# Golden weights in four pieces, constants moved, expert rows added by the gathers

## The chip, the cores and the metric

One Trainium2 chip, one of its cores. The metric is device microseconds of one launch; the kernel before takes 431.03 us as the median of three runs (430.78 to 431.78). Times in the text are microseconds from the start of the profiled span unless they say otherwise.

## The reference, cut to what matters

A decoder of two layers over 4 x 256 tokens of width 256. Each layer has an attention, a cross step and a feed-forward step, and after each of them x = layernorm(x + step(x)). Four things matter here.

In the first layer the cross step is a choice of one of four experts by the token's id; only the second half of the tokens (1024 in all, in two halves of 512) is routed through blocks of rows in the kernel:

```
for e in range(E):
    g = silu(einsum('bsd,fd->bsf', hidden_states, Wg[e]))
    u = einsum('bsd,fd->bsf', hidden_states, Wu[e])
    y = einsum('bsf,df->bsd', g * u, Wd[e])
    out = where((expert_ids == e)[..., None], y, out)
```

The feed-forward step of the first layer has eight experts (256 wide), all of them computed for all tokens, and summed by the Golden weights, eight small numbers for each token:

```
inh = sigmoid(x @ Wr / temperature)
in_zone = (inh >= GOLDEN_LOWER) & (inh <= GOLDEN_UPPER)
distance = abs(inh - GOLDEN_CENTER)
weights = exp(-distance / 0.1) * in_zone
no_expert = sum(weights) < 1e-08
fb = exp(-distance / 0.3)
fb_w = fb * (mask of fb's two largest);  fb_w = fb_w / max(sum(fb_w), 1e-08)
weights = where(no_expert, fb_w, weights)
weights = weights / max(sum(weights), 1e-08)
out = einsum('bte,betd->btd', weights, e_out)
```

The second layer's attention works in groups of 32 tokens, its cross step is a masked attention over ctx (the mask is one of the constants below), and its feed-forward step has eight routed experts of 176 and a shared one.

## The kernel before, in words

**Tiles.** Tokens lie in eight tiles of 128 (x_tok, 128 partitions x 256 each), four tiles to a half (HT = 4). Every matmul operand is kept as two float32r parts, high and low, and a product is three matmuls: high x high, high x low, low x high. So each weight pack (pk_raw, loaded by SyncE) is rounded by ScalarE into pk_hi and the rest is taken by GpSimd into pk_lo; each hidden block (hraw) goes the same way into h_hi and h_lo.

**Units and slots.** A unit is one expert for one half of the tokens: units 0 to 3 are the four experts of the first layer's cross step (first half of the tokens), 4 to 11 the Golden experts for the first half, 12 to 19 those for the second half. Each unit has two slots of 128 hidden rows; slot 8 is the first of unit 4. For a slot TensorE makes the gate product (step g, 6 matmuls of 128x512) and the up product (step u, also 6); ScalarE takes the Silu (s, L1233); VectorE multiplies (m, L1888); ScalarE rounds (h, L1247); GpSimd subtracts (l, L1489). After two slots TensorE makes the down product (d, 24 matmuls of 128x256, L877 to L879) into banks 4 and 5, and VectorE adds it to x_tok with the unit's weights (a, four instructions, L1902). ScalarE and GpSimd convert a unit's gate and up weights in step G (L1265, L1495) and its down weights in step D (L1276, L1500).

**The waits around it.** u of a slot waits for m of two slots earlier, since it writes the bank that this m reads. g waits for the Silu of two slots earlier. d waits for the low halves of both of its slots and, bank by bank, for the two adds of the unit before it that read this bank. A pack's high half waits until TensorE has used the buffer it goes to.

**Orders.** Each engine runs a list written out by hand (PE_ORDER, ACT_ORDER, POOL_ORDER, DVE_ORDER, SP_ORDER): a name of a step and its number, in program order. There is no other scheduling; an engine that waits holds all that is behind it. r0.i and r1.i are the steps of the Golden routing for the first and second half: 0 the layernorm's statistics, 2 the transposes' low parts, 3 the logits, 4 the distance (VectorE) and the two exps (ScalarE), 5 the whole of the Golden weights (VectorE, gold_weights). gold_weights is a chain of small instructions (128x32 or 128x4), each linked to the one before by a semaphore: zone, near weights, the two largest with their masks (top2), the fallback, the sum of both. Its result gold is read by the adds a4 and later (first half), a12 and later (second half). Its neighbours in DVE_ORDER are m9 and m10 in the first half and m24 and m25 in the second.

**The cross step's blocks.** The second half's tokens are sorted by expert into seven blocks of 128 rows in DRAM (xs_dram) by indirect DMAs (steps P), go through the experts block by block (steps x1.0j to x1.4j, x1.4j being the statistics of the first half's tiles), and lie in ys_dram. Four indirect DMAs, issued by GpSimd (steps Q, x0_fetch), gather each token's row into o_tok; VectorE adds a tile of them to x_tok and takes the layernorm's statistics (x1.50 to x1.53). k1 to k4 are the small VectorE steps that compute the slots; k4 makes the list of the blocks' experts, which TensorE reads ahead of x1.10.

**Constants.** Step c (later_constants, L1766 to L1770) casts the pad mask to float (128x1024), takes its maximum, scales it, and makes bk_four; the first reader is the second layer's attention.

Of the kernel before, what the change touches and what calls it, by code (L numbers as in the profile page):

```python
# [183 lines left out]
e0.10 e1.10 m24 r1.5 m25 e0.12 e1.12 m26 c a0.3 a12 a0.4 m27 a0.5 a0.6 m28 a0.7 m29 a0.8 a13 m30 a0.9 a0.10 a14 m31
a0.25 m32 m33 a0.11 e0.0 a15 a0.26 e1.0 m34 a16 e0.2 e1.2 m35 e0.3 e1.3 m36 e0.4 e1.4 m37 e0.5 e1.5 m38 a17 m39 e0.7
e1.7 a18 a0.22 a19 e2.10 e3.10 a0.23 m40 e2.12 e3.12 a1.3 a1.4 m41 m42 a1.5 a1.6 a1.7 a1.8 o43 m43 a1.9 o44 m44 a1.10
a1.25 o45 m45 o46 m46 a1.11 o47 m47 a1.26 e2.0 e3.0 o48 m48 e2.2 e3.2 e2.3 e3.3 o49 m49 o50 m50 e2.4 e3.4 e2.5 e3.5
o51 m51 o52 m52 e2.7 e3.7 o53 m53 a1.22 a1.23 m54 x0 m55 m56 o57 m57 o58 y0 m58 o59 m59 o60 m60 o61 m61 o62 m62 o63
m63 o64 m64 o65 m65 o66 m66 o67 m67 w0 w1 z1
""".split()  # L190


def decoder_program(nc, x_rows, x_cols, ids, pad_mask, w_attn0, w_attn1, bias_cols, bias_rows, bias_v1, bias_o,
                    w_route, temperature, consts, pk_x0, pk_f0, pk_x1, pk_f1, cw_dram, xs_dram, ys_dram, out):
    with ExitStack() as ctx:
# [3 lines left out]
        def sem(name):  # L199
# [1206 lines left out]
        def _(pool):  # L1406
# [189 lines left out]
        def _(dve):  # L1596
# [75 lines left out]
            def per_token(v):  # L1672
                return v.unsqueeze(2).to_broadcast([P, HT, E0])
# [64 lines left out]
            def x0_expert(stage, j):  # L1738
# [12 lines left out]
                elif stage == 2:  # L1751
                    dve.wait_ge(sems["x0_hh"], j + 1)
                    TT(h0_cols(h_lo, j), x0_bank(2, j).rearrange("p (c t) -> p c t", c=KC),
                       h0_cols(h_hi, j).bitcast(F32), ALU.subtract).then_inc(sems["x0_hl"], 1)
                elif stage == 4:
                    dve.wait_ge(sems["acc_done"], 4 * (EX - 1) + j + 1)
                    link(dve.bn_stats(stats[:, j, :], x_tok[:, j, :]))
                else:
                    T = HT + j
                    dve.wait_ge(sems[f"x0_got{j // 2}"], 32)  # L1760
                    TT(x_tok[:, T, :], x_tok[:, T, :], o_tok[:, j, :], ALU.add).then_inc(sems["x0_added"], 1)
                    dve.wait_ge(sems["x0_added"], j + 1)
                    link(dve.bn_stats(stats[:, j, :], x_tok[:, T, :]))
# [178 lines left out]
            def golden(i, h):  # L1942
# [7 lines left out]
                elif i == 4:  # L1950
# [296 lines left out]
```

## Time and profile before

| | |
|---|---|
| median of three runs | 431.03 us |
| the profiled execution | 432.45 us |
| its span | 430.4 us |
| mean granted clock of TensorE | 0.992 |
| busy: PE / PEld / DVE / ACT / POOL | 95% / 82% / 60% / 56% / 63% of the span |
| chain that ended last | PE 71%, DVE 14%, ACT 5%, issue 4%, POOL 2%, DMA 2% |

PE is TensorE (PEld its weight loads), DVE VectorE, ACT ScalarE, POOL GpSimd; L12 is line 12 of the kernel. A timeline row gives start, duration and, in brackets, how long the engine had been idle and what released it. An instruction that stands in its engine waiting for a resource, and not for a semaphore, shows this as a longer duration. A matmul's end is modelled: the row of a product that follows on can begin a little before the one ahead has ended. The granted clock is the share of the 2.4 GHz level that TensorE was given. The profile comes from one execution, so a sum made in it is made against 432.45 us.

### The profile page before, as it was taken

Reading aid. Unit: us, or ns where it says so; the run is one execution under the profiler, and the core shown is the slowest. Engines: PE = TensorE matmul, PEld = TensorE weight load, DVE = VectorE, ACT = ScalarE, POOL = GpSimd, SP = SyncE. Lnnn points to the kernel's source line nnn. Section 1 sums busy time; section 2 is a strip of 40 time slices with the busy share of each in tenths; the row PEclk is TensorE's granted clock in tenths of the full one; section 3 lists DMA queues with packets and bytes.
Section 4 is the critical chain, followed back from the end, with each engine's and each line's share of the span. In section 5 each row is a group of like instructions: output and inputs, shape, how many; then the busy total and the mean of one; then the engine's idle time right before and its main releaser. Section 6 shows DMA issues by size and latency. Waiting matters only on the chain.

```text
span 430.4 us, 9389 instructions
## 1 busy us (share of the span) xinstructions
PE 409.0 (95%) x3615; PEld 354.7 (82%) x3615; DVE 257.2 (60%) x652; ACT 239.6 (56%) x429; POOL 271.3 (63%) x251
## 2 busy tenths in 40 slices
PE   8999999995999999899989999999989999999994
PEld 6888979884889888788878899798768989888983
DVE  5868757529836348966644587656445676363243
ACT  4846664673384775352733757672635757544543
POOL 2744484374598577575867548457757386877763
PEclk9999999999999999999999999999999999999998
DMA  7843022413023313042232102222532332554412
GB/s 248 288 143 116 36 68 80 148 51 122 0 79 124 105 61 124 24 126 96 76 89 76 38 0 84 68 98 62 145 116 75 115 104 79 155 161 151 140 31 99
DMA packets 22855, 43.09 MB, mean 100 GB/s; under 512 B 3051, under 2 KB 10347, under 8 KB 22812
## 3 DMA queue, kind: packets, MB, share of 16 engines
q1 hardware_dynamic: 21708, 40.92, 30.2%
q0 software_dynamic: 384, 1.05, 0.7%
q8 instruction: 29, 0.48, 0.5%
q10 hardware_dynamic: 720, 0.53, 0.4%
q14 instruction: 14, 0.11, 0.1%
HBM read 38.52 MB, written 3.44 MB: 97 GB/s over the span
## 4 chain that ended last, share of the span: by engine, by line
PE 71%; DVE 14%; ACT 5%; issue 4%; POOL 2%; DMA 2%; SPq 0%; DVEq 0%; POOLq 0%; ACTq 0%
PE bank L548 12%; PE bank L549 11%; PE bank L551 11%; PE bank L877 6%; PE bank L879 6%; PE bank L878 6%; PE bank L957 3%; DVE hraw L1888 2%; PE bank L896 2%; PE bank L945 1%; DMA q_buf<-x_cols_dram 1%; DVE x_tok L1902 1%; POOL rstd L1419 1%; PE bank L571 1%; PE bank L927 1%
## 5 line engine op out<-in xcount | busy, mean ns | idle before, releaser
L1489 POOL TENSOR_TENSOR h_lo<-hraw,h_hi 128x512 fp32r<-128x512 f32 x68 | 87.7, 1293 | 65.7 <-ACT h_hi L1247 65.5
L548 PE MATMUL bank<-xT_hi,pk_hi 128*128 128x512 f32 x240 | 97.8, 408 | 6.3 <-DVE hraw L1888 6.3
L549 PE MATMUL bank<-xT_hi,pk_lo 128*128 128x512 f32 x240 | 95.2, 397 | 0.6 <-issue 0.6
L1247 ACT ACTIVATE h_hi<-hraw 128x512 fp32r<-128x512 f32 x68 | 42.8, 629 | 75.3 <-DVE hraw L1888 75.2
L551 PE MATMUL bank<-xT_lo,pk_hi 128*128 128x512 f32 x240 | 76.0, 398 | 0.0
L1495 POOL TENSOR_TENSOR pk_lo<-pk_raw,pk_hi 128x512 fp32r<-128x512 f32 (+1 forms) x44 | 74.6, 1695 | 1.5 <-ACT pk_hi L1265 1.3
L1888 DVE TENSOR_TENSOR hraw<-bank,sil 128x512 f32<-128x512 f32 x68 | 46.9, 689 | 47.1 <-ACT sil L1233 22.6
L877 PE MATMUL bank<-pk_hi,h_hi 128*128 128x256 f32 x240 | 68.9, 287 | 0.2
L879 PE MATMUL bank<-pk_hi,h_lo 128*128 128x256 f32 x240 | 67.8, 283 | 0.0
L878 PE MATMUL bank<-pk_lo,h_hi 128*128 128x256 f32 x240 | 67.8, 282 | 0.0
L548 PEld LDWEIGHTS bank<-xT_hi,pk_hi 128*128 128x128 f32 x240 | 45.6, 190 | 17.2 <-DVE hraw L1888 7.2
L1500 POOL TENSOR_TENSOR pk_lo<-pk_raw,pk_hi 128x256 fp32r<-128x256 f32 (+1 forms) x44 | 41.9, 952 | 20.5 <-ACT pk_hi L1276 20.5
L551 PEld LDWEIGHTS bank<-xT_lo,pk_hi 128*128 128x128 f32 x240 | 45.4, 189 | 11.1 <-DVE xT_lo L1650 0.3
L549 PEld LDWEIGHTS bank<-xT_hi,pk_lo 128*128 128x128 f32 x240 | 45.7, 190 | 9.6 <-issue 0.9
L877 PEld LDWEIGHTS bank<-pk_hi,h_hi 128*128 128x128 f32 x240 | 45.8, 191 | 1.8 <-issue 0.9
L878 PEld LDWEIGHTS bank<-pk_lo,h_hi 128*128 128x128 f32 x240 | 45.8, 191 | 0.8
L879 PEld LDWEIGHTS bank<-pk_hi,h_lo 128*128 128x128 f32 x240 | 45.8, 191 | 0.0
L1276 ACT ACTIVATE pk_hi<-pk_raw 128x256 fp32r<-128x256 f32 (+1 forms) x44 | 21.5, 489 | 32.4 <-PE bank L879 32.3
L1265 ACT ACTIVATE pk_hi<-pk_raw 128x512 fp32r<-128x512 f32 (+1 forms) x44 | 34.2, 777 | 8.5 <-DMA pk_raw<-pk_f_dram 4.8
L1419 POOL TENSOR_TENSOR rstd<-var_e,mhalf 128x2 f32<-128x2 f32 (+1 forms) x19 | 15.3, 806 | 30.9 <-DVE var_e L1619 22.1
L1902 DVE SCALAR_TENSOR_TENSOR x_tok<-bank,gold,x_tok 128x256 f32<-128x256 f32 x64 | 27.2, 476 | 10.3 <-PE bank L879 10.2
L1233 ACT ACTIVATE sil<-bank 128x512 f32<-128x512 f32 x46 | 27.0, 587 | 6.1 <-PE bank L551 6.0
(306 smaller groups left out, 808.6 us busy)
## 6 DMA issues: line engine op xcount, KB each, us to landing
pk_raw<-pk_f_dram SPq DMA_DIRECT2D x28, 384.0 KB, 3.1
pk_raw<-pk_f_dram SPq DMA_DIRECT2D x16, 512.0 KB, 3.6
pk_raw<-pk_f_dram SPq DMA_DIRECT2D x16, 256.0 KB, 3.3
kv_buf<-pk_x_dram SPq DMA_DIRECT2D x4, 512.0 KB, 3.6
x_tok<-x_rows_dram SPq DMA_DIRECT2D x1, 1024.0 KB, 9.4
pk_raw<-pk_x_dram SPq DMA_DIRECT2D x4, 256.0 KB, 5.8
brow<-cw_dram SPq DMA_DIRECT2D x4, 256.0 KB, 3.2
cw_late<-cw_dram SPq DMA_DIRECT2D x4, 256.0 KB, 3.4
```

Source lines behind the costliest of these rows:

```text
L548: pe.matmul(o, w(kc)[0], x(kc)[0], start=kc == 0, stop=False)
L549: pe.matmul(o, w(kc)[1], x(kc)[0], start=False, stop=False)
L551: m = pe.matmul(o, w(kc)[0], x(kc)[1], start=False, stop=kc == KC - 1)
L877: pe.matmul(o, hh, vh, start=first, stop=False, skip_group_check=True)
L878: pe.matmul(o, hh, vl, start=False, stop=False, skip_group_check=True)
L879: m_ = pe.matmul(o, hl, vh, start=False, stop=closed and t % 2 == 1 and kc == chunks - 1, skip_group_check=True)
L1247: A(h_hi[:, row, at * 512:(at + 1) * 512], hraw[:, s % 2, :], ACT.Copy).then_inc(sems["hid_hi"], 1)
L1265: A(g_part(kind, i, pk_hi), raw, ACT.Copy).then_inc(sems["g_hi"], 1)
L1489: pool.tensor_tensor(h_lo[:, row, q], hraw[:, s % 2, :], h_hi[:, row, q].bitcast(F32), ALU.subtract).then_inc(sems["hid_lo"], 1)
L1495: pool.tensor_tensor(g_part(kind, i, pk_lo)[:, 0:w], raw_g(kind, i)[0][:, 0:w], g_part(kind, i, pk_hi)[:, 0:w].bitcast(F32), ALU.subtract) ...
L1500: pool.tensor_tensor(d_part(kind, i, pk_lo), raw_d(kind, i)[0], d_part(kind, i, pk_hi).bitcast(F32), ALU.subtract).then_inc(sems["d_lo"], 1)
L1888: TT(hraw[:, r, :], other[:, :], sil[:, r, :], ALU.mult).then_inc(sems["hid_mul"], 1)
```

## The change

The Golden weights are cut into four pieces on VectorE: zone goes to the end of step 4, near (with top2) is step 5, fallback step 6 and total step 7. In the first half near stays between m9 and m10, fallback and total go behind x1.50 and x1.51, and a4 goes from behind x1.50 to behind m13. In the second half the three pieces go from between m24 and m25 to behind m21, m22 and m23, ahead of a10. The constants (c) go from behind m26 to behind m18, k4 from ahead of a0 to behind m5. On ScalarE the first half's two exps (r0.4) go from behind G2 to ahead of h8. The four gathers add each token's row to x_tok in the DMA (compute_op add), so o_tok, the four VectorE adds and their semaphore fall away; the statistics now wait for the gather alone. The orders of TensorE, GpSimd and SyncE are the same.

```diff
 ACT_ORDER
-... r0.2 x1.36 s8 r0.3 h8 s9 h9 G2 r0.4 s10
+... r0.2 x1.36 s8 r0.3 r0.4 h8 s9 h9 G2 s10
...
 DVE_ORDER
-k3 m1 n1.0 m2 m3 k4 a0 m4 m5 m6 a1 ...
+k3 m1 n1.0 m2 m3 a0 m4 m5 k4 m6 a1 ...
...
-... r0.2 r0.3 m8 r0.4 m9 r0.5 m10 x1.50
-a4 m11 x1.51 m12 x1.52 x1.53 r1.0 m13 m14 a5 a6 m15 m16 m17 r1.2 a7 r1.3 a8 m18 r1.4 m19 m20 a9 m21 m22 m23 a10 a11
-e0.10 e1.10 m24 r1.5 m25 e0.12 e1.12 m26 c a0.3 ...
+... r0.2 r0.3 m8 r0.4 m9 r0.5 m10 x1.50
+r0.6 m11 x1.51 r0.7 m12 x1.52 x1.53 r1.0 m13 a4 m14 a5 a6 m15 m16 m17 r1.2 a7 r1.3 a8 m18 c r1.4 m19 m20 a9 m21 r1.5
+m22 r1.6 m23 r1.7 a10 a11 e0.10 e1.10 m24 m25 e0.12 e1.12 m26 a0.3 ...
...
             def x0_fetch(t):
 
                 pool.wait_ge(sems["x0_ys"], 16 * NB)
-                pool.indirect_dma_start(o_tok[:, t, :], None, ys_dram,
-                                        bass.IndirectOffsetOnAxis(ap=slot_i[:, t:t + 1], axis=0)
-                                        ).then_inc(sems[f"x0_got{t // 2}"], 16)
+                pool.indirect_dma_start(x_tok[:, HT + t, :], None, ys_dram,
+                                        bass.IndirectOffsetOnAxis(ap=slot_i[:, t:t + 1], axis=0),
+                                        compute_op=ALU.add).then_inc(sems[f"x0_got{t // 2}"], 16)
...
                     T = HT + j
                     dve.wait_ge(sems[f"x0_got{j // 2}"], 32)
-                    TT(x_tok[:, T, :], x_tok[:, T, :], o_tok[:, j, :], ALU.add).then_inc(sems["x0_added"], 1)
-                    dve.wait_ge(sems["x0_added"], j + 1)
                     link(dve.bn_stats(stats[:, j, :], x_tok[:, T, :]))
...
-            def gold_weights(h):
+            def gold_zone(h):
 
                 q = slice(HT * h, HT * (h + 1))
                 dve.wait_ge(sems["rt_dist"], h + 1)
                 link(TS(zone[:, q, :], inh[:, q, :], float(GOLD_LO), None, ALU.is_ge))
                 link(STT(pick[:, q, :], inh[:, q, :], float(GOLD_HI), zone[:, q, :], ALU.is_le, ALU.mult))
+
+            def gold_near(h):
+
+                q = slice(HT * h, HT * (h + 1))
                 dve.wait_ge(sems["rt_exp"], h + 1)
                 link(TT(wz[:, q, :], wz[:, q, :], pick[:, q, :], ALU.mult))
                 total(s1[:, q], wz[:, q, :])
                 link(TS(none_in[:, q], s1[:, q], 1e-8, None, ALU.is_lt))
                 top2(fb, h)
+
+            def gold_fallback(h):
+
+                q = slice(HT * h, HT * (h + 1))
                 link(TT(fb[:, q, :], fb[:, q, :], pick[:, q, :], ALU.mult))
                 total(s2[:, q], fb[:, q, :])
                 link(TS(s2[:, q], s2[:, q], 1e-8, None, ALU.max))
                 link(dve.reciprocal(s1[:, q], s2[:, q]))
                 link(TT(fb[:, q, :], fb[:, q, :], per_token(s1[:, q]), ALU.mult))
                 link(TT(fb[:, q, :], fb[:, q, :], per_token(none_in[:, q]), ALU.mult))
+
+            def gold_total(h):
+
+                q = slice(HT * h, HT * (h + 1))
                 link(TS(s2[:, q], none_in[:, q], -1.0, 1.0, ALU.mult, ALU.add))
                 link(TT(wz[:, q, :], wz[:, q, :], per_token(s2[:, q]), ALU.mult))
                 link(TT(wz[:, q, :], wz[:, q, :], fb[:, q, :], ALU.add))
...
                     STT(dist[:, q, :], inh[:, q, :], float(GOLD_C), zone[:, q, :], ALU.subtract, ALU.max
                         ).then_inc(sems["rt_dist"], 1)
+                    gold_zone(h)
                 elif i == 5:
-                    gold_weights(h)
+                    gold_near(h)
+                elif i == 6:
+                    gold_fallback(h)
+                elif i == 7:
+                    gold_total(h)
```

## Rows read from the trace of the kernel before

**Rows 1.** TensorE's timeline (start us, duration us, engine, line, operation, [idle before it and releaser]).

```profile
95.25 0.36 PE L877 MATMUL bank<-pk_hi,h_hi 128*128 128x256 f32 x1
...
106.33 0.80 PE L548 MATMUL bank<-xT_hi,pk_hi 128*128 128x512 f32 x1 [5.17 <-DVE hraw L1888]
...
114.86 0.28 PE L877 MATMUL bank<-pk_hi,h_hi 128*128 128x256 f32 x1
```

**Rows 2.** Busy time by window: start:end, length, PE, PEld, DVE, ACT, POOL, granted clock, DMA.

```profile
106.30:109.30 3.00, 2.97 (x7) 2.42 (x8) 2.93 (x8) 1.12 (x2) 1.28 (x1) 0.50 0.01 3
```

**Rows 3.** VectorE's timeline around the Golden weights of the first half.

```profile
89.36 0.19 DVE L1954 SCALAR_TENSOR_TENSOR dist<-inh,zone 128x32 f32<-128x32 f32 x1
...
92.27 0.69 DVE L1888 TENSOR_TENSOR hraw<-bank,sil 128x512 f32<-128x512 f32 x1 [2.71 <-ACT sil L1233]
...
96.34 1.07 DVE L1924 TENSOR_TENSOR wz<-wz,pick 128x32 f32<-128x32 f32 x1 [3.07 <-ACT fb L1303]
...
99.28 1.29 DVE L1666 TENSOR_TENSOR pick<-con,top_f 128x32 f32<-128x32 f32 x1
...
101.27 2.10 DVE L1930 TENSOR_SCALAR s<-s 128x4 f32<-128x4 f32 x1
...
105.58 0.69 DVE L1888 TENSOR_TENSOR hraw<-bank,sil 128x512 f32<-128x512 f32 x1
```

**Rows 4.** GpSimd's timeline in the same stretch.

```profile
94.95 2.40 POOL L1495 TENSOR_TENSOR pk_lo<-pk_raw,pk_hi 128x1024 fp32r<-128x1024 f32 x1
...
99.17 1.35 POOL L1500 TENSOR_TENSOR pk_lo<-pk_raw,pk_hi 128x512 fp32r<-128x512 f32 x1 [1.82 <-ACT pk_hi L1276]
...
101.00 2.34 POOL L1495 TENSOR_TENSOR pk_lo<-pk_raw,pk_hi 128x1024 fp32r<-128x1024 f32 x1 [0.48 <-ACT pk_hi L1265]
```

**Rows 5.** Tile o_tok: count, ns min/median/max, first and last start us.

```profile
L1446 POOL DMA_INDIRECT o_tok<-ys_dram,slot_i x4: 947/950/1082, 86.1 to 90.0; - x4
...
L1761 DVE TENSOR_TENSOR x_tok<-x_tok,o_tok x4: 414/415/1491, 106.2 to 112.2; 128x256 f32<-128x256 f32 x4
...
DMA to landing us min/median/max: 1.7/1.9/2.7
```

**Rows 6.** VectorE's timeline, 141 to 159.

```profile
141.16 0.25 DVE L1953 TENSOR_SCALAR zone<-inh 128x32 f32<-128x32 f32 x1
...
153.47 0.69 DVE L1888 TENSOR_TENSOR hraw<-bank,sil 128x512 f32<-128x512 f32 x1 [2.33 <-ACT sil L1233]
...
155.40 0.69 DVE L1888 TENSOR_TENSOR hraw<-bank,sil 128x512 f32<-128x512 f32 x1 [1.24 <-ACT sil L1233]
...
158.77 0.88 DVE L1902 SCALAR_TENSOR_TENSOR x_tok<-bank,gold,x_tok 128x256 f32<-128x256 f32 x2 [0.72 <-PE bank L879]
```

**Rows 7.** GpSimd's timeline, 145 to 157.

```profile
145.27 1.29 POOL L1489 TENSOR_TENSOR h_lo<-hraw,h_hi 128x512 fp32r<-128x512 f32 x1 [2.06 <-ACT h_hi L1247]
...
156.85 1.29 POOL L1489 TENSOR_TENSOR h_lo<-hraw,h_hi 128x512 fp32r<-128x512 f32 x1 [0.65 <-ACT h_hi L1247]
```

**Rows 8.** ScalarE's timeline, the high half of weight pack 3.

```profile
99.86 1.06 ACT L1265 ACTIVATE pk_hi<-pk_raw 128x1024 fp32r<-128x1024 f32 x1 [0.77 <-PE bank L551]
```

**Rows 9.** VectorE's timeline, the constants (first and last of four).

```profile
177.37 0.69 DVE L1766 CAST cap<-mask_w 128x1024 f32<-128x1024 uint8 x1
...
180.07 2.24 DVE L1770 TENSOR_SCALAR bk_four<-con,bcol 128x4 f32<-128x4 f32 x1
```

**Rows 10.** TensorE's timeline, 147 to 176.

```profile
147.19 0.28 PE L877 MATMUL bank<-pk_hi,h_hi 128*128 128x256 f32 x1
...
160.18 0.36 PE L877 MATMUL bank<-pk_hi,h_hi 128*128 128x256 f32 x1
...
175.51 0.50 PE L548 MATMUL bank<-xT_hi,pk_hi 128*128 128x512 f32 x1 [1.15 <-DVE hraw L1888]
```

**Rows 11.** VectorE's timeline, the multiply m4.

```profile
55.54 0.69 DVE L1888 TENSOR_TENSOR hraw<-bank,sil 128x512 f32<-128x512 f32 x1
```

**Rows 12.** ScalarE's timeline, the Silu s4.

```profile
54.86 0.58 ACT L1233 ACTIVATE sil<-bank 128x512 f32<-128x512 f32 x1
```

More of the change, by code:

```diff
@@ L158 @@
 s4 h4 s5 h5 G1 s6 h6 D1 s7 h7 x1.00 x1.01 x1.10 x1.02 x1.11 x1.20 x1.03 x1.12 x1.21 x1.04 x1.30 x1.13 x1.22 x1.05
-x1.31 x1.14 x1.23 x1.06 x1.32 x1.15 x1.24 x1.33 x1.16 x1.25 x1.34 x1.26 x1.35 r0.2 x1.36 s8 r0.3 h8 s9 h9 G2 r0.4 s10
+x1.31 x1.14 x1.23 x1.06 x1.32 x1.15 x1.24 x1.33 x1.16 x1.25 x1.34 x1.26 x1.35 r0.2 x1.36 s8 r0.3 r0.4 h8 s9 h9 G2 s10
 D2 G3 h10 s11 h11 s12 h12 s13 h13 s14 D3 G4 r1.1 h14 s15 S0 D4 G5 h15 s16 h16 s17 r1.2 h17 D5 G6 D6 s18 r1.3 h18 s19
@@ L180 @@
 k0 p2 b0.0 b0.1 b0.2 b0.3 b0.4 b0.5 k1 b1.0 b0.6 b0.7 b1.1 b0.8 p5 b1.2 n0.0 b1.3 b1.4 b1.5 b1.6 b1.7 n0.2 b1.8 k2 m0
-k3 m1 n1.0 m2 m3 k4 a0 m4 m5 m6 a1 m7 a2 x1.00 x1.01 a3 x1.10 x1.02 x1.11 x1.20 x1.03 x1.40 x1.12 x1.21 x1.04 x1.41
+k3 m1 n1.0 m2 m3 a0 m4 m5 k4 m6 a1 m7 a2 x1.00 x1.01 a3 x1.10 x1.02 x1.11 x1.20 x1.03 x1.40 x1.12 x1.21 x1.04 x1.41
 x1.13 x1.22 x1.05 x1.42 x1.14 x1.23 x1.06 x1.43 r0.0 x1.15 x1.24 x1.16 x1.25 x1.26 r0.2 r0.3 m8 r0.4 m9 r0.5 m10 x1.50
-a4 m11 x1.51 m12 x1.52 x1.53 r1.0 m13 m14 a5 a6 m15 m16 m17 r1.2 a7 r1.3 a8 m18 r1.4 m19 m20 a9 m21 m22 m23 a10 a11
[L184 to L189, printed above, removed]
+r0.6 m11 x1.51 r0.7 m12 x1.52 x1.53 r1.0 m13 a4 m14 a5 a6 m15 m16 m17 r1.2 a7 r1.3 a8 m18 c r1.4 m19 m20 a9 m21 r1.5
+m22 r1.6 m23 r1.7 a10 a11 e0.10 e1.10 m24 m25 e0.12 e1.12 m26 a0.3 a12 a0.4 m27 a0.5 a0.6 m28 a0.7 m29 a0.8 a13 m30
+a0.9 a0.10 a14 m31 a0.25 m32 m33 a0.11 e0.0 a15 a0.26 e1.0 m34 a16 e0.2 e1.2 m35 e0.3 e1.3 m36 e0.4 e1.4 m37 e0.5 e1.5
+m38 a17 m39 e0.7 e1.7 a18 a0.22 a19 e2.10 e3.10 a0.23 m40 e2.12 e3.12 a1.3 a1.4 m41 m42 a1.5 a1.6 a1.7 a1.8 o43 m43
+a1.9 o44 m44 a1.10 a1.25 o45 m45 o46 m46 a1.11 o47 m47 a1.26 e2.0 e3.0 o48 m48 e2.2 e3.2 e2.3 e3.3 o49 m49 o50 m50
+e2.4 e3.4 e2.5 e3.5 o51 m51 o52 m52 e2.7 e3.7 o53 m53 a1.22 a1.23 m54 x0 m55 m56 o57 m57 o58 y0 m58 o59 m59 o60 m60
+o61 m61 o62 m62 o63 m63 o64 m64 o65 m65 o66 m66 o67 m67 w0 w1 z1
 """.split()
@@ L312, in decoder_program @@
             x0_t_ps x0_xh x0_xl x0_g_ps x0_silu x0_mul x0_v_ps x0_hh x0_hl x0_d_ps x0_y x0_ys
-            x0_got0 x0_got1 x0_added""".split()
+            x0_got0 x0_got1""".split()
         for n in names:
```

## The prediction

> **How the profile is read.** Steps are named as in the order lists: g and u are a slot's gate and up products on TensorE, d a unit's down product, s the Silu and h the high half on ScalarE, m the multiply and a the adds of a unit on VectorE, l the low half on GpSimd, G and D a weight pack's two conversions (ScalarE, then GpSimd). All moments are those of the trace before.
>
> **What bounds the kernel now.** TensorE is busy 95% of the span, so only its holes can be won. Its timeline has one large hole: u12 begins at 106.33, 5.17 us after g12 ended, and the releaser is the VectorE multiply m10 [rows 1]. The window behind it shows the granted clock at 0.50 for 3.0 us, the 1.2 GHz level [rows 2]; against the 2.4 GHz level that is another 1.5 us. So the hole costs up to 6.7 us in all. From u12 to d5 five products take 8.53 us [rows 1], 7.03 at full clock, 1.41 each.
>
> The hole is the Golden weights of the first half, one piece on VectorE between m9 and m10: from 96.34 to 105.58 [rows 3]. These are 128x32 instructions of 0.19 us, but three of them last 1.07, 1.29 and 2.10 us. Put beside GpSimd's timeline the reason shows: each ends 0.03 to 0.06 us after a GpSimd subtraction ends (97.35, 100.52, 103.34) [rows 4]. An instruction of VectorE that works from SBUF to SBUF waits for the GpSimd instruction that is running; what reads PSUM, and the reductions and searches, did not wait in this trace. I call it a lock. Behind the third stall ten instructions take 2.21 us, so 0.22 each. That prices the new pieces: fallback (6 instructions) 1.3 us, total (7) 1.5, near what is left, 9.24 less the stalls 3.9 less 2.8, so 2.5.
>
> **The change part by part.**
>
> *The adding gathers.* Four VectorE adds go: 0.41 us each, the longest 1.49 because of a lock [rows 5]. That is 2.7 us of VectorE time between 106 and 114. The gathers are issued on GpSimd at 86.1 to 90.0, 0.95 us each, and landed 1.7 to 2.7 us after issue [rows 5]. VectorE asks for them at x1.50, at 99 at the earliest, so their landing may grow by 5 us unseen. What an adding gather costs GpSimd to issue no row shows. The nearest row is the plain one, so 0.95, taken as unchanged; the upper bound is twice that, since it has two operands per row; below nothing there is no reason to go. The queue behind them is l8, l9 and pack 2. The Trainium skill, "Collectives: The Full Stack", section "The bandwidth ceiling: the fold count and why AG ≠ RS ≠ AR", says that the add inside a DMA is free but that it reads two sources and so needs twice the read descriptors. By that page the issue could reach the upper bound, and the time would be that of the rival on the gathers below; no row here shows it.
>
> *The exps ahead of h8 on ScalarE.* They wait for dist, which ends at 89.55 [rows 3], and take two times 0.2 (estimate, the size of that row); h8 could start at about 89.3. So h8, s9 and m9 come 0.65 us later: m9 at 92.9 instead of 92.27. A low half starts 1.45 us after its multiply starts (155.40 to 156.85) [rows 6, 7] and lasts 1.3, so l9 ends at 95.65, and d4, at 95.25 before [rows 1], starts 0.4 later. The fewer table switches are off the path.
>
> *Near, fallback, total of the first half.* Near runs from 93.5. Its first instructions and the searches last to 95.3, the copy waits for l9 (95.65), the next instruction for pack 2's subtraction right behind it (2.40 us [rows 4]), so to 98.05, and near ends at 98.5. m10 takes 98.5 to 99.2; u12 wants it at 101.55. So the hole of 5.17 us and the slow clock go: five products on, d5 could start at 108.6 instead of 114.86, a gain of 6.3.
>
> What is late next? d5 needs half of a4, since a4 frees its bank, and a4 now stands behind fallback, total and m13. The statistics of x1.50 (0.4, like the add of that size) bring VectorE to 99.6. Then GpSimd runs D2 (99.55 to 100.9), pack 3 (101.4 to 103.75, because its ScalarE half starts at 99.86 [rows 8] plus 0.4) and l10 (to 105.0). If fallback meets all three, it ends at 105.05 and m11 with it, 0.7 us too late even for its own start; u13 stands 1.4 us. Total meets l11 (1.45 us behind m11) and ends at 108.75; u14 stands 0.9. Behind m12 come two statistics, the aggregation, l12's lock, m13 at 111.7 and half of a4 (0.88): d5 at 113.25, gain 1.6. If fallback slips ahead of D2 and pack 3, and here 0.05 us decide it, then m11 comes by 103.8, m12 at 107.5, d5 at 112.0, gain 2.9. Between them I take 2.3. VectorE and u14 absorb the 0.4 of d4 in either case.
>
> *Constants moved (c).* Before they ran from 177.37, three instructions in 2.70 us, the fourth then locked to 2.24 [rows 9]; what they cost there was hidden behind d12, so I win nothing. In the new place they stand between m18 and r1.4, which began at 141.16 [rows 6]: 2.7 + 0.2, a short lock of 0.2, then r1.4 0.4 and zone 0.4 put m19 at 145.1. Before, l19 at 145.27 [rows 7] puts m19 at 143.8. l19 now ends at 147.85, and d9, which reads it, began at 147.19 [rows 10]: 0.7 us lost (between 0 and 1.2).
>
> *Near, fallback, total of the second half.* Before they stood behind m24 and cost one wait of 1.15 us before u27 [rows 10]; this goes. Now they stand between m21, m22, m23 and a10. m21 starts at 153.47 [rows 6], near at 154.1; its copy waits for l21 (to 156.2), m22 at 156.8 instead of 155.40. Fallback from 157.4; its last instruction can't pass l22 (158.25 to 159.55), m23 at 159.8. Total from 160.4 meets l23 (161.25 to 162.55) and ends at about 163.1. Only then comes a10, which before began at 158.77 and whose first half takes 0.88 [rows 6]: 164.0. d11 waits for just this half (it began at 160.18 [rows 10]); queued behind d11 on TensorE is everything. Loss 3.7 us; without any lock a10's half is done at 161.5, loss 1.3.
>
> *k4 behind m5.* Its 0.8 us leave the place ahead of m4. But m4 began at 55.54 [rows 11] and its Silu ended at 55.44 [rows 12]: at most 0.1 us, taken as nothing. Behind m5 its cover is the wait for the next Silu; TensorE reads the block list some 10 us later.
>
> **Sum.** -2.3 + 0.7 + 3.7 - 1.15 = +0.95 us. The profiled execution took 432.45, its span 430.4, 2.05 around it; it lies 1.42 above the median. 432.45 + 0.95 = 433.4 there, 432.0 for the median.
>
> **The rivals.** About 0.2%, 0.86 us, is what a measurement can tell from no change.
> - *The pieces meet no locks.* Then near ends at 96.0, m11 hangs only on pack 3, h10 and s11 on ScalarE (102.6), m12 comes at 105.15, half of a4 at 108.7 and d5 at once: -6.1. Second half: +0.5 + 1.3 - 1.15. Together -5.45: 425.6. For it: every lock is a meeting of two timelines that both shift. Against it: GpSimd stands in subtractions for most of 94 to 106, and l follows each m by 1.45 us wherever the pieces lie.
> - *Only the second half is free of locks* (decided by whether l21 to l23 fall on searches and reductions): -2.3 + 0.65 = -1.65: 429.4. Against it: fallback's last instruction starts 1.7 us behind its multiply, inside l22.
> - *The clock falls in d11's wait.* TensorE would stand 3.7 us, and the granted clock fell here after 5.17 us of standing and not after 1.15. If it falls as before, 1.5 us more: 433.5.
> - *The adding gathers hold GpSimd.* From an issue time of 1.4 us up (four times 0.45 is l9's room) they decide: at 1.9 each, l9 ends at 97.4, d4 starts 2.1 us late, of which the later waits give back some 0.6: 433.5.
> - *m10 stays late* and the hole stays, with nothing moved: 431.0.
>
> **How the numbers follow.** Forecast 0.44, of it 0.20 within 0.2% and 0.24 slower, since 0.95 lies just beyond the 0.86; no locks 0.12; second half free 0.17; clock 0.13; gathers 0.12; m10 late 0.02. Faster: 0.12 + 0.17 = 0.29. Within: 0.20 + 0.02 = 0.22. Slower: 0.24 + 0.13 + 0.12 = 0.49. Leaving out the rival without locks (0.12) and some 0.08 at the top, where two of the slower ones meet, the range is 427.8 to 434.4. The forecast alone, by its bounds (first half -2.9 to -1.6, c 0 to 1.2, d11 3.4 to 4.0, less 1.15), spans 430.4 to 433.5.
>
> **What would show it.** Right: no wait before u12 and no window at 0.50 there; waits before u13, u14 and d5 that sum to some 4 us, released by m11, m12 and x_tok adds; a new wait of 3 to 4 us before d11, released by x_tok; none of 1.15 before u27; the longest small VectorE instructions still end with GpSimd subtractions. Wrong: the gathers at over 1.4 us on GpSimd, a d11 that starts behind d10, or a wait for the gathers' landing at x1.50.

## The result, and the profile after

| | before | after |
|---|---|---|
| median | 430.9 us (4 runs, 430.7 to 431.8) | 437.06 us (4 runs, 436.39 to 438.85) |
| ratio, 95% interval | | 1.0145 (1.0111 to 1.018) |
| profiled execution, its span | 432.45, 430.4 | 436.39, 434.4 |
| mean granted clock | 0.992 | 0.990 |

The change costs 6.2 us; 1 us was forecast and the range ended at 434.4. Of all the executions one, the profiled one of experiment 6, ran at a mean granted clock of 0.845 and took 452.36 us; it is left out.

First the two traces must be laid on each other. I call the changed kernel after. In its trace everything on TensorE runs 1.08 us earlier from the first product that waits for loaded weights on; nothing of the change lies ahead of it, and the other kernels below spread over the same range (8.86 to 10.07). The row of before, then that of after (start, duration):

```profile
10.07 0.47 PE L628 MATMUL bank<-wa_hi,xT_hi 128*128 128x512 f32 x1
```

```profile
8.99 0.47 PE L628 MATMUL bank<-wa_hi,xT_hi 128*128 128x512 f32 x1
```

So every moment of after is compared with that of before plus 1.08, and I call the difference the lag. By the spans the change costs 4.0 + 1.08 = 5.1 us in these two executions; before's profiled execution lies 1.5 above its median, and its start, the latest of all, may be the larger part of that.

TensorE's timeline of after, its waits of 0.4 us and more between 90 and 200 us (in brackets how long it was idle, and the releaser):

```profile
95.13 0.35 PE L877 MATMUL bank<-pk_hi,h_hi 128*128 128x256 f32 x1 [0.77 <-POOL h_lo L1489]
...
101.45 0.50 PE L548 MATMUL bank<-xT_hi,pk_hi 128*128 128x512 f32 x1 [0.41 <-DVE hraw L1886]
...
105.98 0.50 PE L548 MATMUL bank<-xT_hi,pk_hi 128*128 128x512 f32 x1 [1.47 <-DVE hraw L1886]
...
109.65 0.50 PE L548 MATMUL bank<-xT_hi,pk_hi 128*128 128x512 f32 x1 [0.61 <-DVE hraw L1886]
...
113.25 0.36 PE L877 MATMUL bank<-pk_hi,h_hi 128*128 128x256 f32 x1 [1.93 <-DVE x_tok L1900]
...
146.26 0.36 PE L877 MATMUL bank<-pk_hi,h_hi 128*128 128x256 f32 x1 [0.44 <-issue]
...
165.11 0.55 PE L877 MATMUL bank<-pk_hi,h_hi 128*128 128x256 f32 x1 [5.87 <-DVE x_tok L1900]
```

In order these are d4, u12, u13, u14, d5, d9 and d11. The hole of 5.17 us before u12 [rows 1] is gone, and a hole of 5.87 us stands before d11. The granted clock around both places (start:end, length, busy time of PE, PEld, DVE, ACT, POOL, clock, DMA):

```profile
110.00:113.40 3.40, 1.47 (x7) 0.93 (x6) 3.33 (x11) 1.80 (x4) 2.81 (x4) 1.00 0.00 0
113.40:116.50 3.10, 3.10 (x26) 3.06 (x27) 2.06 (x6) 0.11 (x2) 0.97 (x1) 1.00 0.00 0
164.75:168.00 3.25, 2.89 (x13) 2.92 (x14) 1.00 (x3) 0.00 (x0) 2.83 (x2) 0.50 0.76 246
168.00:171.00 3.00, 3.00 (x17) 2.86 (x16) 1.41 (x4) 0.47 (x1) 0.00 (x0) 0.65 0.48 175
```

The clock stays up at d5 and falls to the 1.2 GHz level behind d11's wait: d11 lasts 5.3 us instead of 3.1.

The lag along the span: +0.96 at d4; -0.53 at d5, where -2.3 was forecast; +0.15 at d9; and behind d11 (+5.9 for its wait, +2.2 for the clock) +8.2 at g24. Then it shrinks: 0.4 at the transposes ahead of u26, 1.4 at u27, where before waited 1.15 us [rows 10], 0.5 up to g28, and 0.8 over the last 250 us, where the traces differ in short waits, most of them marked issue. That leaves 5.1.

The gathers of after, by their line (count, ns min/median/max, first and last start), beside [rows 5]:

```profile
L1446 POOL DMA_INDIRECT x_tok<-ys_dram,slot_i x4: 1546/1556/1674, 85.1 to 90.8; - x4
...
DMA to landing us min/median/max: 3.7/3.8/3.9
```

An adding gather holds GpSimd for 1.55 us where a plain one took 0.95. DMA packets between 84 and 100 us, before and then after (packets, MB, share):

```profile
q0 software_dynamic: 192, 0.52, 10.5%
```

```profile
q0 software_dynamic: 576, 0.52, 22.6%
```

The same bytes go in three times the packets. In before they are 128 packets of 4 KB and 64 small ones, in after 512 of 1 KB, each a token's row by itself, and the same 64.

Behind the last one, GpSimd's and then VectorE's timeline:

```profile
90.77 1.55 POOL L1446 DMA_INDIRECT x_tok<-ys_dram,slot_i  x1 [0.30 <-issue]
91.76 3.12 POOL L1489 TENSOR_TENSOR h_lo<-hraw,h_hi 128x512 fp32r<-128x512 f32 x2
94.27 2.95 POOL L1495 TENSOR_TENSOR pk_lo<-pk_raw,pk_hi 128x1024 fp32r<-128x1024 f32 x1
```

```profile
92.13 5.16 DVE L1926 TENSOR_TENSOR wz<-wz,pick 128x32 f32<-128x32 f32 x1
...
99.15 1.29 DVE L1666 TENSOR_TENSOR pick<-con,top_f 128x32 f32<-128x32 f32 x1
...
100.70 0.69 DVE L1886 TENSOR_TENSOR hraw<-bank,sil 128x512 f32<-128x512 f32 x1
...
101.76 1.55 DVE L1934 TENSOR_TENSOR fb<-fb,pick 128x32 f32<-128x32 f32 x1
```

Near's first multiply, 0.18 us of work, lasts 5.16 and ends with the third subtraction in a row, l8, l9 and pack 2's. One of near's later instructions then meets D2's subtraction (1.29 us at 99.15), and m10 starts at 100.70.

Total in the second half, VectorE and then GpSimd:

```profile
160.49 1.25 DVE L1948 TENSOR_SCALAR s<-s 128x4 f32<-128x4 f32 x1
161.77 0.18 DVE L1949 RECIPROCAL s<-s 128x4 f32<-128x4 f32 x1
161.99 2.07 DVE L1950 TENSOR_TENSOR gold<-wz,s 128x32 f32<-128x32 f32 x1
164.09 1.66 DVE L1900 SCALAR_TENSOR_TENSOR x_tok<-bank,gold,x_tok 128x256 f32<-128x256 f32 x4
```

```profile
160.45 1.27 POOL L1489 TENSOR_TENSOR h_lo<-hraw,h_hi 128x512 fp32r<-128x512 f32 x1 [1.74 <-ACT h_hi L1247]
161.67 2.34 POOL L1495 TENSOR_TENSOR pk_lo<-pk_raw,pk_hi 128x1024 fp32r<-128x1024 f32 x1
```

The first long one waits for l23, which I had foreseen. The last instruction of total waits for the weight pack's subtraction right behind l23, which I had not, and a10, the fourth row, stands behind it.

### The profile page after: what moved, and what is told of

It reads as the page before. It is cut to its first block, busy times and chain, and to the rows that moved or that the text cites. A ratio compares the mean times of both kernels' runs of the same rounds, so it can differ in the third digit from the quotient of the medians.

```text
span 434.4 us, 9385 instructions
## 1 busy us (share of the span) xinstructions
PE 409.6 (94%) x3615; PEld 355.3 (82%) x3615; DVE 261.5 (60%) x648; ACT 238.1 (55%) x428; POOL 272.8 (63%) x251
## 4 chain that ended last, share of the span: by engine, by line
PE 59%; DVE 7%; issue 3%; ACT 2%; DMA 1%; SPq 1%; POOL 1%; POOLq 0%; DVEq 0%; ACTq 0%
PE bank L548 11%; PE bank L549 10%; PE bank L551 10%; PE bank L877 6%; PE bank L879 6%; PE bank L878 6%; PE bank L957 2%; PE bank L945 1%; PE bank L571 1%; PE bank L896 1%; DVE hraw L1886 1%; DMA brow<-cw_dram 1%; PE bank L927 1%; PE bank L928 1%; PE bank L929 1%
## 5 line engine op out<-in xcount | busy, mean ns | idle before, releaser
L877 PE MATMUL bank<-pk_hi,h_hi 128*128 128x256 f32 x240 | 70.2, 293 | 9.2 <-DVE x_tok L1900 7.8
L878 PE MATMUL bank<-pk_lo,h_hi 128*128 128x256 f32 x240 | 68.8, 287 | 0.0
L879 PE MATMUL bank<-pk_hi,h_lo 128*128 128x256 f32 x240 | 68.7, 286 | 0.0
L877 PEld LDWEIGHTS bank<-pk_hi,h_hi 128*128 128x128 f32 x240 | 46.8, 195 | 11.8 <-issue 11.0
L878 PEld LDWEIGHTS bank<-pk_lo,h_hi 128*128 128x128 f32 x240 | 46.9, 196 | 0.7
L879 PEld LDWEIGHTS bank<-pk_hi,h_lo 128*128 128x128 f32 x240 | 46.9, 195 | 0.0
```

The costliest lines, as they stand in the source:

```text
L877: pe.matmul(o, hh, vh, start=first, stop=False, skip_group_check=True)
L878: pe.matmul(o, hh, vl, start=False, stop=False, skip_group_check=True)
L879: m_ = pe.matmul(o, hl, vh, start=False, stop=closed and t % 2 == 1 and kc == chunks - 1, skip_group_check=True)
```

## The experiments

Each was timed beside the kernel before on the same chip; the median of before was 431.2 us for experiments 1 to 4, 431.8 for 5 to 8 and 432.0 for the others. Single runs of one kernel spread by 1 to 1.5%, so mechanisms are read from traces and lags, and medians decide only where their interval allows.

**1. The second half's pieces back behind m24.**

```diff
-m21 r1.5 m22 r1.6 m23 r1.7 a10 a11 e0.10 e1.10 m24 m25
+m21 m22 m23 a10 a11 e0.10 e1.10 m24 r1.5 r1.6 r1.7 m25
```

> The changed kernel with the second half's near, fallback and total behind m24 again; the rest of the change stays. Theory (the second half's place costs the 6 us): the wait of 5.87 us before d11 and the 2.2 us at the 0.50 clock behind it go, the wait of 1.15 us before u27 comes back: 437.1 - 5.9 - 2.2 + 1.15 = 430.2 us, and the trace shows d11 directly behind d10 and no window at 0.50. Rival (the first half and the gathers cost what is lost, and d11's wait only takes the place of later ones): 434 us or more.

Measured: 430.31 us, ratio 0.9964 (0.9937 to 0.999), so 7.8 us less than after by the two ratios. d11 follows d10 without a wait, and the clock is 1.00 there. The first half's waits repeat after's to 0.02 us (0.77, 0.40, 1.48, 0.61, 1.92). Two things came out otherwise. The wait before u27 did not return: zone was done earlier, and the small instruction that lasted 1.27 us before, because it met l24, now came ahead of l24 and ended with the memset in front of it:

```profile
169.09 0.39 DVE L1928 TENSOR_SCALAR none_in<-s 128x4 f32<-128x4 f32 x1
```

```profile
169.13 0.33 POOL L1565 MEMSET kv_buf<- 128x128 f32 x1
169.49 1.30 POOL L1489 TENSOR_TENSOR h_lo<-hraw,h_hi 128x512 fp32r<-128x512 f32 x1
```

And the clock fell at d5, behind the very waits behind which it stayed up in after:

```profile
113.40:116.50 3.10, 3.10 (x16) 3.10 (x17) 1.57 (x4) 0.22 (x1) 1.11 (x1) 0.55 0.00 0
```

That costs 1.57 us here. The theory holds: the second half's place is what the change loses by.

**2. Plain gathers in the changed kernel.** The diff of x0_fetch and of the add, undone.

> The changed kernel with plain gathers into o_tok and VectorE's four adds again; everything else of the change stays. Theory (an adding gather holds GpSimd 0.6 us longer, four of them push l8, l9 and the pack's subtraction 2.4 us back, and near's first multiply waits for all three): the gathers take 0.95 us, l9 ends near 94.3, near's first multiply takes 0.2 us, m10 starts by 97.5 instead of 100.7, the waits before d4 and u12 (0.76 and 0.41) go and those before u13, u14 and d5 (4.0 in sum) shrink by 1 to 2: 434 us, between 433 and 435.5. Rival (the adds on VectorE cost what the shorter gathers give): 436.5 to 437.5 us.

Measured: 438.8 us, ratio 1.0182 (1.0145 to 1.0219), no better than after. The theory's first part is right: the gathers take 0.95 us and near's first multiply 0.18. VectorE:

```profile
92.89 0.18 DVE L1928 TENSOR_TENSOR wz<-wz,pick 128x32 f32<-128x32 f32 x1
...
95.09 2.33 DVE L1665 TENSOR_TENSOR zone<-con,top_f 128x32 f32<-128x32 f32 x1
...
97.78 0.69 DVE L1888 TENSOR_TENSOR hraw<-bank,sil 128x512 f32<-128x512 f32 x1
...
110.36 1.48 DVE L1761 TENSOR_TENSOR x_tok<-x_tok,o_tok 128x256 f32<-128x256 f32 x1
```

The waits before d4 and u12 are gone, and u13 is 1.3 us ahead of after by the lag. But the adds, one of them locked to 1.48 us, bring a4 so late that d5 waits 3.26 us and starts 0.4 us later than in after. The theory's second part, 434 us, failed. The rival's mechanism was right, though the time lies above its range too (437.5). So in this order the adding gathers save VectorE's 2.7 us and win 0.4 of them at d5: in the trace they take back about 2.3. The medians can't tell the two kernels apart.

**3. The adding gathers alone, in the kernel before.**

> The kernel before with the adding gathers alone. Theory: GpSimd's queue is 2.4 us later, so d4 waits 1 to 2 us for l9, and m10 comes up to 2.4 us later behind the same locks: 430.9 + 1.5 to 2.5 = 432.4 to 433.4 us, the wait before u12 at 5 us still. Rival (the longer issue is covered, and four adds of 0.41 us less behind m10 win): 430.0 to 430.9 us.

Measured: 433.45 us, ratio 1.0056 (1.002 to 1.0092), 2.2 us above before by the medians, as the theory had it. The exps are still late there, but zone now meets the subtractions:

```profile
92.11 5.43 DVE L1919 TENSOR_SCALAR zone<-inh 128x32 f32<-128x32 f32 x1
```

u12's wait is 5.61, and d4's 0.76, less than the 1 to 2 of the theory. The lag is 1.3 at u12 and 2.6 at d5. The second 1.3 is the clock, which is 0.50 from 106.3 to 112.3 here, while in before it is 0.50 up to 109.3 and 0.96 over the next 3 us. It need not come from the edit: in the traces of 9 and 10, whose kernels are before's up to this place, the clock stayed down longer too, for 1.3 and 0.9 us of lag. The interval of the ratio, 0.9 to 4.0 us, is clear of zero. Alone, the edit is a loss; where a wait for VectorE's adds sets the end, as in 2, it is paid back.

**4. The constants back behind m26.**

```diff
-m18 c r1.4 ... m25 e0.12 e1.12 m26 a0.3
+m18 r1.4 ... m25 e0.12 e1.12 m26 c a0.3
```

> The changed kernel with the constants (c) back behind m26. Theory: m19 and l19 come 2.2 us earlier, the wait of 0.44 us before d9 goes and with it 0.7 us of the end: 436.4 us. Rival (d9's wait is only taken over by a10 and d11, which hang on VectorE's pieces whose start is set by the exps and m20 and not by c): 437.1 us, unchanged, with d11's wait longer by 0.5 us.

Measured: 437.65 us, ratio 1.0156 (1.0119 to 1.0193): unchanged. The trace shows why both were half right. d9 waits for nothing, and the lag is 0.6 less at its start and 0.7 behind it; d11's wait is 5.85, not longer, so the 0.7 is kept up to there. It is too small for the medians, and the slow clock behind d11 cost 1.3 us here against 2.2 in after, a spread larger than the effect.

**5. a10 ahead of the second half's total.**

```diff
-m23 r1.7 a10 a11
+m23 a10 r1.7 a11
```

> The changed kernel with a10 ahead of the second half's total (near and fallback stay between m21, m22 and m23). Theory (d11 waits for a10 only because total and its two waits for GpSimd, 4.5 us in all, stand ahead of it): a10 starts at 159.7, 0.1 us behind m23, d11 0.9 us later at 160.6, so its wait is 1.4 instead of 5.87 us; the clock stays at 1.00 there (2.2 us), and u27 waits for nothing: 437.1 - 4.5 - 2.2 = 430.4 us. Rival (total's place only hands the wait on: a11 and the statistics for the next example come later and d12 or u27 wait 3 us or more): 433 us or more.

Measured: 436.24 us, ratio 1.011 (1.0058 to 1.0162). The theory failed and the rival held. d11's wait fell to 2.56 us, not to 1.4, and hangs on l23 now, since fallback's lock had already put m23 back. Total moved fully into GpSimd's row of pack subtractions, VectorE then GpSimd:

```profile
162.59 0.55 DVE L1944 TENSOR_SCALAR s<-none_in 128x4 f32<-128x4 f32 x1
163.18 2.35 DVE L1945 TENSOR_TENSOR wz<-wz,s 128x32 f32<-128x32 f32 x1
165.56 1.22 DVE L1946 TENSOR_TENSOR wz<-wz,fb 128x32 f32<-128x32 f32 x1
...
167.03 2.08 DVE L1948 TENSOR_SCALAR s<-s 128x4 f32<-128x4 f32 x1
```

```profile
163.08 2.40 POOL L1495 TENSOR_TENSOR pk_lo<-pk_raw,pk_hi 128x1024 fp32r<-128x1024 f32 x1
165.44 1.29 POOL L1500 TENSOR_TENSOR pk_lo<-pk_raw,pk_hi 128x512 fp32r<-128x512 f32 x1
166.69 2.40 POOL L1495 TENSOR_TENSOR pk_lo<-pk_raw,pk_hi 128x1024 fp32r<-128x1024 f32 x1
```

Seven small instructions take 7.0 us, each long one ending with a subtraction (the first, 0.55, with l23's). a11 and the statistics behind it come late, and the transposes of the next step wait 2.72 us. The clock is 1.00 behind d11's wait, but it fell at d5, as in 1, and behind the transposes' wait (0.50 over 176.10:179.50). Taking one consumer out from behind the pieces is not enough; the place itself is bad.

**6. a4 directly behind m12.**

```diff
-m12 x1.52 x1.53 r1.0 m13 a4 m14
+m12 a4 x1.52 x1.53 r1.0 m13 m14
```

> The changed kernel with a4 directly behind m12, ahead of the statistics and m13. Theory (d5's wait of 1.93 us is VectorE's order, not the weights themselves): a4's half ends at 109.6 + 0.9 = 110.5, u14 ends at 111.3, so d5 starts directly behind u14 and the wait of 1.93 goes; m13 comes 1.6 us later, which has 3 us of cover behind d5: 437.1 - 1.9 = 435.2 us. Rival (g15 and u15 then wait for m13, or r1.2 for the statistics): the 1.9 us come back within the next three products and the time is 437.1 us.

Measured: 436.08 us, ratio 1.0069 (1.0038 to 1.01), against after's 1.0145 that is 3.3 us less, with a resolution of about 2. It agrees with the theory (1.9 us) and not with the rival; its trace is not read here, so what became of d5's wait is not shown.

**7 and 8. All in one: second half and c back, and the first half in an order that puts each multiply ahead of the piece that would delay it**, with adding and with plain gathers. Zone and the exps keep their new places.

```diff
-m10 x1.50 r0.6 m11 x1.51 r0.7 m12 x1.52 x1.53 r1.0 m13 a4 m14
+m10 x1.50 m11 r0.6 m12 r0.7 a4 x1.51 x1.52 x1.53 r1.0 m13 m14
```

> The changed kernel with the second half behind m24 again, c behind m26 again, and the first half in the order m10 x1.50 m11 r0.6 m12 r0.7 a4 x1.51 x1.52 x1.53 r1.0 m13. Theory (each multiply goes ahead of the piece that would delay it): d4 and u12 keep their waits of 0.76 and 0.41, u13 and u14 lose theirs (1.47 and 0.60), a4's half ends near 110.4 and d5 starts there instead of 113.25, 2.8 us earlier; d9's 0.44 goes too: against the kernel with the second half back (430.3) 427.0 us, or 425.5 if the clock doesn't fall at d5 as it did there for 1.6 us. Rival (fallback and total meet l11 and l12 in the new order and a4 comes as late as before): 430 us.

> The same order with plain gathers and VectorE's four adds. Theory (plain gathers let l9 end at 94.3 and m10 start near 97.0, and the adds now stand behind a4, where VectorE has room): no wait before d4, u12, u13 and u14, d5 starts near 109.5: 0.9 us below the adding version, 426.1 us. Rival (the first add still stands ahead of m11, and an add of 0.41 us locked to 1.49 puts m11 or a4 back): equal to the adding version or up to 1 us above it.

Measured: 428.31 us, ratio 0.9913 (0.988 to 0.9945), and 427.28 us, ratio 0.9906 (0.9874 to 0.9939). Both beat both kernels; which of them is better the medians don't tell. They lie 1.3 and 1.2 us above what the theories said (427.0 and 426.1). In the traces u13 and u14 wait for nothing, and d5 still waits 1.82 us in either, for a4, because total meets l12; it has a lag of -3.0 (adding) and -4.1 (plain). The clock fell at d5 with adding gathers (window 0.53, 1.6 us) and stayed with plain ones.

**9 and 10. The lock by itself.** In the kernel before, between a9 and m21:

```diff
+for _ in range(8): link(TT(pick[:, 0:HT, :], wz[:, 0:HT, :], wz[:, 0:HT, :], ALU.mult))
```

and, in the other, eight of

```diff
+link(dve.tensor_reduce(s1[:, 0:HT], wz[:, 0:HT, :], axis=AXX, op=ALU.add))
```

> The kernel before with eight chained 128x32 multiplies (SBUF to SBUF, result unused) on VectorE between a9 and m21, where it was idle for 2.33 us while GpSimd ran two subtractions back to back (151.03 to 152.32, 152.27 to 153.56). Theory (a two-operand VectorE instruction waits for GpSimd's running subtraction, and one gets in at each boundary): the first lasts 1.1 us, the second 1.25, the other six 0.19 each; m21 starts near 155.0 instead of 153.47. Rival (there is no such lock, the long ones were waits for data): all eight last 0.19, 1.8 us in all, and m21 stays where it was.

> The kernel before with eight chained 128x32 reductions (one operand, SBUF, result unused) in the same place. Theory (reductions don't take part in the lock): all eight last 0.19 us beside the two running subtractions, 1.8 us in all, and m21 starts at its old place. Rival (every SBUF access waits): the first two last 1.1 and 1.25 us as the multiplies do.

Measured (one run each, 434.26 and 432.31 us), VectorE and GpSimd with the multiplies (x8 is a run of eight, its time the sum with gaps), then VectorE with the reductions:

```profile
151.28 3.76 DVE L1767 TENSOR_TENSOR pick<-wz 128x32 f32<-128x32 f32 x8
155.07 0.69 DVE L1892 TENSOR_TENSOR hraw<-bank,sil 128x512 f32<-128x512 f32 x1
```

```profile
151.25 1.36 POOL L1500 TENSOR_TENSOR pk_lo<-pk_raw,pk_hi 128x512 fp32r<-128x512 f32 x1 [2.11 <-ACT pk_hi L1276]
152.57 1.29 POOL L1489 TENSOR_TENSOR h_lo<-hraw,h_hi 128x512 fp32r<-128x512 f32 x1
```

```profile
150.80 1.73 DVE L1767 TENSOR_REDUCE s<-wz 128x4 f32<-128x32 f32 x8
153.34 0.69 DVE L1892 TENSOR_TENSOR hraw<-bank,sil 128x512 f32<-128x512 f32 x1 [0.81 <-POOL h_lo L1489]
```

Eight multiplies take 3.76 us: the first, which starts together with GpSimd's subtraction, 0.18, the next two 1.16 and 1.22, each to the end of a subtraction, the others 0.19; eight reductions in the same place 1.73, the longest 0.19. The theory stands to 0.2 us in the whole, with the waits one place later in the row. The Trainium skill, "SBUF — State Buffer", section "Who interferes with whom", has the rule: a VectorE instruction with two SBUF inputs contends with a GpSimd instruction that reads SBUF, a reduction never does on this chip. These two runs agree with it.

**11. Near behind the last adding gather instead of during it.** Four chained reductions (result unused) between m9 and r0.5 of the changed kernel.

> The changed kernel with four chained reductions (result unused) ahead of near, so that near's first multiply comes at 93.0 instead of 92.1, behind the end of the last adding gather (92.3) and inside l8. Theory (behind an adding gather GpSimd's next subtractions overlap in the records by 0.6 us, so there is no boundary for VectorE to get in at): the multiply still ends at 97.2, with the pack's subtraction, and lasts 4.2 us. Rival (only an instruction that is queued while the gather is issued is passed over): it gets in at the end of l8, 93.6, and lasts 0.6 us.

Measured (one run, 435.65 us):

```profile
93.00 4.27 DVE L1930 TENSOR_TENSOR wz<-wz,pick 128x32 f32<-128x32 f32 x1
```

It ends at 97.27, at the same subtraction's end: the rival falls. In all seven traces with adding gathers that are read here, the three subtractions behind the last gather overlap in GpSimd's records (in after l8 is recorded from 91.76, while the gather runs to 92.32; the pack's from 94.27 though l9 ends at 94.88), and the waiting instruction is passed over at both boundaries. In the three with plain gathers and an early near (2, 8 and 12) near's multiply comes after l8 has ended and meets nothing; l9 and the pack's subtraction follow one another, and one VectorE instruction gets in between them. That the overlap is the reason is likely, not shown. The Trainium skill, "Perfetto Trace Analysis", section "DMA Instruction — SWDGE (GPSIMD)", bears on it: two of GpSimd's processors write the descriptors of a DMA and the profile's end is that of the last one, which would leave the others free to begin l8; no run here shows the processors apart.

**12. Fallback in two, and a5 ahead of m14, on top of 8.**

```diff
-m10 x1.50 m11 r0.6 m12 r0.7 a4 x1.51 x1.52 x1.53 r1.0 m13 m14 a5 a6
+m10 x1.50 r0.6 m11 r0.8 m12 r0.7 a4 x1.51 x1.52 x1.53 r1.0 m13 a5 m14 a6
```

Here r0.6 is fallback's multiply, sum and lower bound, r0.8 its other three instructions.

> The best_plain kernel with fallback in two (multiply, sum and lower bound ahead of m11, where VectorE was idle for 2.87 us; the other three behind it) and a5 ahead of m14. Theory: the first part's multiply meets the half pack (to 99.5), its other two run before pack 3 begins (100.1), so m11 stays at 101.2; m12 comes 1 us earlier, a4's half ends near 108.0 and d5 starts directly behind u14 at 107.8 instead of 109.55; d6's wait of 1.14 us goes: 1.7 + 1.1 below best_plain, a ratio of 0.984 to 0.986 to the kernel before. Rival (the first part is locked behind pack 3 too, to 102.5): m11 comes 1.3 us later, d5 is at 109.5 again, and only d6's 1.1 us is won: 0.988.

Measured: 426.78 us, ratio 0.9885 (0.9848 to 0.9921), the best of all, though not beyond the interval of 8. The first part slipped in ahead of pack 3 and m11 stayed at 101.60, as the theory wants. Yet d5 still waits, 1.28 us instead of none:

```profile
102.97 1.21 DVE L1945 TENSOR_TENSOR fb<-fb,none_in 128x32 f32<-128x32 f32 x1
104.23 0.69 DVE L1888 TENSOR_TENSOR hraw<-bank,sil 128x512 f32<-128x512 f32 x1
104.83 0.58 DVE L1950 TENSOR_SCALAR s<-none_in 128x4 f32<-128x4 f32 x1
105.45 0.19 DVE L1951 TENSOR_TENSOR wz<-wz,s 128x32 f32<-128x32 f32 x1
105.67 1.33 DVE L1952 TENSOR_TENSOR wz<-wz,fb 128x32 f32<-128x32 f32 x1
```

The second part met the end of pack 3's subtraction (0.53 us at 102.41) and l10, and total met l11 and l12, which themselves came earlier because their multiplies did. d6's wait went from 1.14 to 0.43, but 0.45 came in behind it. The value measured is that of the rival, by another way.

## Why the prediction was wrong, point by point

Three terms of the sum failed. The first half's gain of 2.3 us was 0.5, for the larger part because the gathers' issue was taken as unchanged at 0.95 us. The second half's loss of 3.7 us was 5.9, because total was laid beside l23 and not beside the subtraction behind it. And the clock was to stay up in that wait, and fell for 2.2 us.

**What bounds the kernel: right.** The hole of 5.17 us and its slow clock were the Golden weights held up by GpSimd. The lock is shown by 9 and 10.

**The adding gathers: the step that failed first.** I took the issue as unchanged at 0.95 us, with twice that as the bound and 1.4 as the point from which it decides. It is 1.55. By itself this made GpSimd's queue only a little late: on before's clock l9 ended at 95.96 and the pack's subtraction at 98.30, each 0.3 later than forecast, since the queue had room: GpSimd was idle for 1.42 us ahead of l9 in before. What the sum did not have is that near's first multiply would get in at neither boundary between the three subtractions. Only near's last instructions were to stand behind the pack's; here all that follows the first multiply did, and so near also met D2's. m10 came at 100.70, which is 101.8 on before's clock, instead of 98.5. In 2, with plain gathers, the pack's subtraction ends 0.7 us earlier than in after by the lag, and m10 starts 3.8 us earlier. I gave this rival 0.12 and priced it at 1.5 us, by a late l9 and d4; alone the edit measures +2.2 us (3), but d4 is only 0.6 later than forecast. The Trainium skill's rule on twice the read descriptors, "Collectives: The Full Stack", section "The bandwidth ceiling: the fold count and why AG ≠ RS ≠ AR", was quoted in the prediction and spoke for a longer issue. No run here shows the reads: the bytes of the software queue are the same, and its packets are more because each row goes by itself.

**The exps ahead of h8: right.** They ran at 88.54 to 88.88 and m9 came 0.3 us later than before by the lag (0.65 forecast).

**Near, fallback, total of the first half: mechanism right, size wrong.** In the late case, where fallback meets all the subtractions, the waits before u13, u14 and d5 were forecast at 1.4, 0.9 and 2.4 us; they are 1.47, 0.61 and 1.93. But d5 starts at 113.25, 114.33 on before's clock, where I had 112.0 to 113.25: a gain of 0.5 instead of 2.3. Of the 1.8 us that are missing, 0.7 is that the late case came, and 1.1 lies beyond it. Of the 1.1, 1.0 is there at u12 already: 0.6 from d4's longer wait for l9, 0.4 from u12's wait for m10, both the gathers'. With plain gathers and the adds back (2), d5 is at 114.75 on before's clock; less the adds' 2.7 that is 112.05, the early end of my bounds. That is an estimate, since without the adds the pieces would meet other subtractions; by it the forecast for d5 would have held with gathers that cost nothing. No run shows it.

**Constants: right.** 0.7 us lost at d9 and just behind it (0.6 at its start), 0.7 forecast; 4 gives it back there.

**Second half: mechanism right, one term missing.** d11 was to wait 3.7 us and waits 5.87. Total was to meet l23 and end 0.55 us behind it. I left out that GpSimd goes straight from l23 into pack 8's subtraction, and total's last multiply met that one for 2.07 us. The prediction's own rule, to lay each piece on GpSimd's timeline, was not carried past the next low half. Experiment 5 shows the same row of subtractions taking 5.5 us from the same seven instructions.

**The clock in d11's wait: the rival, and dearer.** Put at 0.13 and 1.5 us; it fell, and cost 2.2 (1.3 in 4). At 5.9 us of standing it fell in all four traces that had such a hole (after, 2, 4 and 11); behind 3.26 us in 2 (d5) it stayed up. What it would have done at the 3.7 us forecast no run shows.

**The wait before u27: right by 1.15 us**, though 1 shows that it goes even with the pieces in their old place.

**k4: nothing, as said.** From the first product to d4's wait the lag stays within 0.04 us.

**The sum.** In the trace, from the forecast lag of 0.95: first half +1.8, total's second lock +2.2, clock +2.2, and -2.0 for what came back behind g24 (3.1 instead of the 1.15 before u27) give 5.2; measured 5.1. On the medians the same 5.2 gives 436.2 and 437.06 was measured. The 0.9 between them no trace accounts for; single runs of one kernel differ by more. Two of the three were rivals on the list, priced one at a time. They are not independent: what comes late makes a longer hole, and behind each hole of 5.2 to 5.9 us in these traces the clock fell. The range cut off the case where they meet. One rival was also priced wrong: with m10 late and the hole still there, the second half's terms stay, +0.7 + 3.7 - 1.15, so it stands at 434.3 and not at 431.0.

## What to carry to other kernels

A chain of small VectorE instructions costs what GpSimd is doing beside it: lay each piece on GpSimd's timeline, and go on past the next subtraction to the end of the row, because one instruction gets in at a boundary and the next one waits again. Place the pieces behind the instruction that TensorE waits for next, not ahead of it, and where GpSimd has a gap; in the second half the old place, one hole of 1.15 us, was 8 us better than the new ones. And an add that moves from VectorE into a gather is not free: here it moved 2.7 us of VectorE into 2.4 us of GpSimd and made a VectorE instruction wait through three subtractions. Alone it lost 2.2 us; beside the other changes its sign is not told by the medians.

## What the runs showed of the hardware

- An adding indirect DMA of 128 rows of 1 KB holds GpSimd 1.55 us, the plain one 0.95, and lands 3.8 us after the start of its issue instead of 1.9 (medians, [rows 5]).
- Behind an adding gather a VectorE instruction was passed over at two boundaries between GpSimd's subtractions (5.16 us for 0.18 of work; 5.43 in experiment 3). Elsewhere one got in at each boundary, as at 162.59, 163.18 and 165.56 in experiment 5.
- A reciprocal and a reduction run beside a GpSimd subtraction in 0.18 and 0.19 us (161.77 in after; experiment 10); a TENSOR_SCALAR on 128x4 waits like a multiply (1.25 us at 160.49).
- The granted clock behind nearly the same waits fell in one execution and not in another: waits of 1.47, 0.61 and 1.93 us ended with 1.00 in after (and in 4 and 11), waits of 1.48, 0.61 and 1.92 us with 0.55 in experiment 1 (and it fell in 5). It stayed at 1.00 behind a wait of 3.26 us (114.50:117.60 in 2) and fell behind one of 2.72 us (0.50 over 176.10:179.50 in 5). What decides it stays open; at d5 it is worth 1.6 us, and part of the spread between runs of one kernel may be this.
